# V transposed in 32x32 blocks by VectorE and reordered through DRAM instead of by TensorE

## The reference

```
xn   = group_norm(x, 32 groups)
q, k = conv1x1+affine(xn): 8 heads of 32 channels each
v4   = conv1x1+affine(xn): 1024 channels, 8 heads of 128
vl   = depthwise 3x3 convolution of v4, then an affine map
attn = q @ k^T * 32**-0.5 + bias[head, |dy|, |dx|]
attn = mix heads with th1 (8x8), softmax over the keys, mix heads with th2 (8x8)
o    = relu(attn @ v + vl)
out  = x + conv1x1+affine(o)
```

## Time and profile before

| | |
|---|---|
| time, median of 3 runs | 4813.72 us (4812.78 to 4814.12) |
| time of the profiled execution | 4811.84 us |
| its span, first to last instruction | 4810.0 us |
| mean granted clock of TensorE | 0.998 |
| busy in the span | PE 4779.1, DVE 4175.9, ACT 3251.4, POOL 988.6 us |
| DMA | 120.23 MB, 7.4% of 16 engines on SP's queue |

### The profile page before, as it was taken

The page is one execution under the profiler, slowest core; times in us unless marked ns, Lnnn a source line. Parts: engine busy times, 40 slices in busy tenths (PEclk is TensorE's granted clock), DMA queues, the critical chain, the costliest instruction groups (busy, mean ns, idle before and its releaser), DMA issues.

```text
span 4810.0 us, 111468 instructions
## 1 busy us (share of the span) xinstructions
PE 4779.1 (99%) x35842; PEld 4760.2 (99%) x35842; DVE 4175.9 (87%) x10897; ACT 3251.4 (68%) x8005; POOL 988.6 (21%) x1093
## 2 busy tenths in 40 slices
PE   7999999999999999999999999999999999999999
PEld 7999999999999999999999999999999999999999
DVE  8888888889888898888888988889888888898887
ACT  6666666666667666667666666766666766666665
POOL 3212212121121221221212212122121221221211
PEclk9999999999999999999999999999999999999999
DMA  1000000000000000000000000000000000000000
GB/s 57 26 20 30 19 26 30 15 30 25 20 30 15 30 25 20 30 15 30 30 15 30 25 20 30 15 30 25 20 30 15 30 29 16 30 21 24 30 15 26
DMA packets 55148, 120.23 MB, mean 25 GB/s; under 512 B 3650, under 2 KB 5842, under 8 KB 55124
## 3 DMA queue, kind: packets, MB, share of 16 engines
q1 hardware_dynamic: 55124, 119.93, 7.4%
HBM read 81.38 MB, written 38.54 MB: 25 GB/s over the span
## 4 chain that ended last, share of the span: by engine, by line
PE 98%; DVE 1%; issue 0%; DMA 0%; ACT 0%; SPq 0%; DVEq 0%
PE psA L250 43%; PE psA L399 14%; PE psL L250 12%; PE psM L250 10%; PE psM L377 8%; PE psL L377 6%; PE psM L367 2%; PE psL L367 2%; DVE psC L620 1%; PE psA L268 0%; PE psA L263 0%; DMA qa<-in_wqkv 0%; DVE probs L675 0%; DVE x_lo L601 0%; DVE q_lo L650 0%
## 5 line engine op out<-in xcount | busy, mean ns | idle before, releaser
L620 DVE SCALAR_TENSOR_TENSOR psC<-vpad,par,psC 128x406 f32<-128x406 f32 x3072 | 1808.7, 637 | 0.0
L498 ACT ACTIVATE probs<-probs,nmax 112x196 f32<-112x196 f32 x1792 | 799.0, 449 | 649.0 <-DVE nmax L675 641.8
L250 PE MATMUL psA<-x_hi,w_lo 128*128 128x392 f32 x2304 | 795.0, 345 | 8.5 <-DVE x_lo L601 8.5
L250 PE MATMUL psA<-x_lo,w_hi 128*128 128x392 f32 x2304 | 788.9, 342 | 0.0
L250 PE MATMUL psA<-x_hi,w_hi 128*128 128x392 f32 x2304 | 788.1, 342 | 0.0
L399 PE MATMUL psA<-qa,shared 105*128 105x196 f32 x4096 | 693.9, 330 | 3.0 <-DVE shared L719 3.0
L399 PEld LDWEIGHTS psA<-qa,shared 105*128 105x128 f32 x4096 | 680.2, 191 | 3.3 <-DVE shared L719 3.3
L650 DVE SCALAR_TENSOR_TENSOR q_lo<-q,th,q_hi 128x392 fp32r<-128x392 f32 x1024 | 604.4, 621 | 34.6 <-ACT q_hi L442 27.6
L719 DVE TENSOR_TENSOR shared<-psA,shared 128x392 f32<-128x392 f32 x512 | 290.1, 567 | 366.5 <-PE psA L399 366.5
L442 ACT ACTIVATE q_hi<-q,th 128x392 fp32r<-128x392 f32 x1024 | 582.0, 620 | 6.0
L434 ACT ACTIVATE o_hi<-shared 128x392 fp32r<-128x392 f32 x512 | 271.5, 530 | 457.6 <-DVE shared L719 457.6
(11 more groups left out here) (85 smaller groups left out, 10500.0 us busy)
## 6 DMA issues: line engine op xcount, KB each, us to landing
xs<-in_x SPq DMA_DIRECT2D x64, 588.0 KB, 3.8
shared<-in_x SPq DMA_DIRECT2D x64, 588.0 KB, 3.8
out<-shared SPq DMA_DIRECT2D x63, 588.0 KB, 3.0
qa<-in_wqkv SPq DMA_DIRECT2D x3, 768.0 KB, 6.7
stage_wp<-in_wp SPq DMA_DIRECT2D x1, 1536.0 KB, 9.9
out<-shared SPq DMA_DIRECT2D x3, 196.0 KB, 2.0
shared<-in_abx SPq DMA_DIRECT2D x1, 165.4 KB
par<-in_par SPq DMA_DIRECT2D x1, 70.5 KB
```

Source lines behind the costliest of these rows:

```text
L250: last = nc.tensor.matmul(dst, w, r, start=(begin and n == 0), stop=(end and n == 2))
L498: nc.scalar.activation(row, row, ACT.Exp, bias=nmax[:, img, b:b + 1], scale=-1.0, accum_out=rowsum[:, img, b:b + 1]).then_inc(s_exp, 1)
L620: nc.vector.scalar_tensor_tensor(a if tap == 7 else sums, src, taps[:, c, TAPS[tap]:TAPS[tap] + 1], a if tap == 0 else sums, MUL, ADD).the ...
```

## The change

TensorE's transposes, their evictions on ScalarE and `ident` are gone; the 14 mixings are left alone in the rotation of the four banks. In their place:

- VectorE runs two STREAM_TRANSPOSE instructions a pair (`turn`), one for an image. Each reads 8 groups of 224 consecutive elements of `vpad` on 128 partitions, transposes every 32x32 block by itself, and writes 1792 elements a partition into `turned` with a step of 8 elements, so that the 8 groups c are innermost. They take the places at which convs(3) stood twice.
- SP sends `turned` to a DRAM scratch `by_key`, 4 transfers for an image, one for each 32 partitions, in runs of 1 KB. When all 4 have landed it brings the rows back, 2 transfers of 112 keys by 4 KB for an image, straight into `vt`. That is 12 transfers a pair, all ahead of the store of the results in SP's order.
- `vt` is now ordered by channel and then by group, so a weight load of attn times V reads 128 elements with a step of 8.
- x_lo, q, k and k_lo share the memory of `turned` (`front`). GpSimd's x_lo of the next pair waits until image 0 has been sent out (s_vt_out[0]).
- ScalarE makes x_hi of the next pair after use 6 of 14 instead of after use 16 of 22.

```diff
@@ SP @@
+            def turned_out(t, img):
+                sp.wait_ge(s_turned, 2 * t + img + 1)
+                rows = by_key[img].rearrange("(b r) a n -> r a b n", r=BLK)
+                for a in range(P // BLK):
+                    sp.dma_start(rows[:, a, :, :],
+                                 turned[a * BLK:(a + 1) * BLK, img, :, :, :].rearrange("p b n c -> p b (n c)")
+                                 ).then_inc(s_vt_out[img], 16)
+
+            def keys_in(t, img):
+                sp.wait_ge(s_vt_out[img], 16 * (P // BLK) * (t + 1))
+                for jc in range(2):
+                    sp.dma_start(vt[0:ROWS, img, jc, :, :].rearrange("p n c -> p (n c)"),
+                                 by_key[img, jc * HALF:jc * HALF + ROWS, :, :].rearrange("k a n -> k (a n)")
+                                 ).then_inc(s_vt_in[img], 16)
...
                     load_x(t + 1)
+                turned_out(t, 0)
+                turned_out(t, 1)
+                keys_in(t, 0)
+                keys_in(t, 1)
                 if not first:
                     store(t)
@@ PE @@
-                for use in range(22):
-                    img, (what, n) = use // 11, USES[use % 11]
-                    bank_free(use)
-                    if what == "vt":
-                        jc, cg = divmod(n, 2)
-                        for c in range(4):
-                            at_ = PITCH + 1 + img * PITCH * PITCH + jc * HALF
-                            mm = nc.tensor.transpose(mix_bank(use)[:, c * P:(c + 1) * P],
-                                                     vpad[:, 4 * cg + c, at_:at_ + HALF], ident[:, :])
-                        mm.then_inc(s_vt_mm, 1)
...
-                    pe.wait_ge(s_vt_sb, 8 * t + 4 * img + 4)
+                    pe.wait_ge(s_vt_in[img], 32 * (t + 1))
                     pe.wait_ge(s_mix_sb, 14 * t + 7 * img + 7)
...
-                                                      vt[0:HALF, img, jc, g * D:(g + 1) * D], attn[:, img, jc, g, :],
+                                                      vt[0:HALF, img, jc, :, g], attn[:, img, jc, g, :],
@@ ACT @@
-                    if use == 16 and not last:
+                    if use == 6 and not last:
                         act.wait_ge(s_v_mm, VT * (t + 1))
                         x_high(t + 1)
@@ DVE @@
+                def turn(img):
+                    at_ = PITCH + 1 + img * PITCH * PITCH
+                    nc.vector.transpose(turned[:, img, :, :, :].rearrange("p b n c -> p c b n"),
+                                        vpad[:, :, at_:at_ + BLOCKS * BLK].rearrange("p c (b k) -> p c b k", b=BLOCKS)
+                                        ).then_inc(s_turned, 1)
...
-                convs(3)
+                turn(0)
                 dve.wait_ge(s_exp, 28 * t + 28)
                 nc.vector.reciprocal(rinv[:, 1, :], rowsum[:, 1, :]).then_inc(s_rinv, 1)
-                convs(3)
+                turn(1)
                 if not first:
                     project_out(t, 2)
                 convs(64)
@@ POOL @@
-                    pool.wait_ge(s_v_mm, VT * (t + 1))
+                    wait_alone(pool, s_vt_out[0], 16 * (P // BLK) * (t + 1))
                     x_low(t + 1)
```

More of the change, by code:

```diff
@@ L19 @@
 HALF = RES // 2 * PITCH
+ROWS = 112
+BLK = 32
+BLOCKS = 7
+PART = VT * BLK
 HR = P // KD
@@ L29 @@
 EPS = 1e-5
+Q_AT = 2 * CT * PIX
+K_HI_AT = Q_AT + QT * COLS
+K_AT = K_HI_AT + QT * COLS
 GAP = 2 * RES * QT * HP - VT // 2 * ACC - 4 * DH
@@ L76, in build @@
         x_hi = sb("x_hi", [P, 2, CT, PIX], f32r)
-        x_lo = sb("x_lo", [P, 2, CT, PIX], f32r)
-        q = sb("q", [P, QT, COLS])
-        k_hi = sb("k_hi", [P, QT, COLS], f32r)
-        k_lo = over("k_lo", [P, QT, COLS])
-        k = sb("k", [P, QT, COLS])
+        x_lo = over("x_lo", [P, 2, CT, PIX])
+        k_hi = over("k_hi", [P, QT, COLS], K_HI_AT)
+        k_lo = over("k_lo", [P, QT, COLS], K_AT)
+        front = sb("front", [P, 2 * BLOCKS * PART])
         q_hi = over("q_hi", [P, 2 * RES, QT, HP])
@@ L156, in build @@
         s_khi, s_klo = sem("s_khi"), sem("s_klo")
+        s_vt_out = [sem("s_vt_out0"), sem("s_vt_out1")]
+        s_vt_in = [sem("s_vt_in0"), sem("s_vt_in1")]
         s_resb, s_rstd, s_xlo, s_mixw = sem("s_resb"), sem("s_rstd"), sem("s_xlo"), sem("s_mixw")
         block = ctx.enter_context(nc.Block())
-        N_PAR_DMA = 7
+        N_PAR_DMA = 6
+        by_key = nc.dram_tensor("by_key", (2, BLOCKS * BLK, P // BLK, PART), f32, kind="Internal").ap()
         def keys(img, b):
@@ L346, in step @@
                     project(t, 2, True)
-                def bank_free(use):
+                for use in range(14):
+                    img, n = divmod(use, 7)
                     if use < 4:
                         pe.wait_ge(s_score, 28 * t + 22 + 2 * use)
-                        return
-                    i, (what, n) = (use - 4) // 11, USES[(use - 4) % 11]
-                    if what == "vt":
-                        pe.wait_ge(s_vt_sb, 8 * t + 4 * i + n + 1)
-                    else:
-                        pe.wait_ge(s_mix_sb, 14 * t + 7 * i + n + 1)
@@ new lines, in step @@
+                    else:
+                        pe.wait_ge(s_mix_sb, 14 * t + use - 3)
+                    pe.wait_ge(s_exp, 28 * t + 14 * img + 2 * n + 2)
+                    pe.wait_ge(s_mixw, 8 * t + 4 * img + group(2 * n + 1) + 1)
+                    bank = mix_bank(use)[:, 0:4 * HP].rearrange("p (j g b i) -> p j g b i", j=2, g=NH, b=2)
+                    for jc in range(2):
+                        for b in range(2):
+                            mm = nc.tensor.matmul(bank[:, jc, :, b, :],
+                                                  probs[0:HP + 1, img, 2 * n + b, jc * HALF:(jc + 1) * HALF],
+                                                  mixw[0:HP + 1, img, 2 * n + b, :].rearrange("p (g i) -> p g i", g=NH),
+                                                  start=True, stop=True)
@@ L502, in step @@
                         conv_centre(t, CENTRES[n])
-                for use in range(22):
-                    img, (what, n) = use // 11, USES[use % 11]
-                    if what == "vt":
-                        jc, cg = divmod(n, 2)
-                        act.wait_ge(s_vt_mm, 8 * t + 4 * img + n + 1)
-                        if use == 0 and not first:
-                            act.wait_ge(s_av_mm, 8 * t)
-                        nc.scalar.copy(vt[0:HALF, img, jc, cg * BANK:(cg + 1) * BANK],
-                                       mix_bank(use)).then_inc(s_vt_sb, 1)
-                    else:
-                        act.wait_ge(s_mix_mm, 14 * t + 7 * img + n + 1)
-                        src = mix_bank(use)[:, 0:4 * HP].rearrange("p (j g m) -> p j g m", j=2, g=NH)
-                        nc.scalar.copy(attn[:, img, :, :, 2 * n * RES:(2 * n + 2) * RES], src).then_inc(s_mix_sb, 1)
-                    if use == 16 and not last:
+                for use in range(14):
+                    img, n = divmod(use, 7)
+                    act.wait_ge(s_mix_mm, 14 * t + use + 1)
+                    if use == 0 and not first:
+                        act.wait_ge(s_av_mm, 8 * t)
+                    src = mix_bank(use)[:, 0:4 * HP].rearrange("p (j g m) -> p j g m", j=2, g=NH)
+                    nc.scalar.copy(attn[:, img, :, :, 2 * n * RES:(2 * n + 2) * RES], src).then_inc(s_mix_sb, 1)
+                    if use == 6 and not last:
                         act.wait_ge(s_v_mm, VT * (t + 1))
```

31 lines of the change are left out of this document (9 added, 22 removed).

## The result

The change makes the kernel slower. Its time is 5282.09 us (median of 4 runs, 5281.4 to 5284.02) beside 4813.92 us for the kernel before on the same chip, a ratio of 1.0974 [1.0955, 1.0993]. The forecast was 4920 us, in a range of 4808 to 5210: the direction is right, the size is not, and the time lies outside the range.

A forecast was written before the change was run, and what follows sets the result against it. TensorE bounds the kernel, with VectorE 3.3 us behind and taking over. VectorE's 0.1 us plus 1.6 us for the clock, times 63 pairs, adds 107 us to 4811.84: 4919, forecast 4920 us, range 4808 to 5210.

The forecast's parts named there:

- the frame: TensorE's saved 3.5 us a pair returns as a 3.6 us stop before u = 2, VectorE binding and the clock falling.
- priced at 1.6 us a pair: Granted clock falls to half behind each TensorE stop, on attn times V and the following tiles: 1.6 us a pair.
- the price of the turn by its length: VectorE's transpose of 1792 elements a partition, priced from a 1536-element row at 1.08 ns an element: 1.94, taken as 2.0 us.
- I take 2.0, by the row nearest in length: Choice of 2.0 us for each VectorE transpose, among rows giving 1.52, 1.94, 2.42 and 6.7 us.
- the forecast's own case: VectorE bounds with a falling clock, transposes of 1.94 to 2.42 us: 4862 to 5040 us, chance 0.42.
- hidden under 166 ns: Attn times V: a 128-column weight load costs 111 ns of pace, covered by 166 ns of matmul, so adds nothing.
- The rival: Attn times V: the step of 8 doubles the weight load to 221 ns, 1.77 us a step; 5085 us, chance 0.11.
- rivals that exclude each other: Slow strided write in VectorE's turn (5240 us, chance 0.17) and slow strided weight load in attn times V (5085 us, 0.11).
- a sign that it is wrong: Forecast called wrong if VectorE still waits for the first product, PE's wait ends on a DMA, or PEclk stays 1.00.
- its own count: Transfers of V: four legs of 4.8 us at 190 GB/s, image 0 in `vt` at 2473.8, in time by 1.6 us.
- The rival of late transfers: V's transfers run at 143 GB/s, 6.4 us a leg, delaying attn times V 4.3 us a pair: 5091 us, chance 0.08.
- The fast case: VectorE's transpose takes 1.52 us and the clock holds, the pair 0.86 us shorter: 4760 us, chance 0.09.

The follow-up runs named there:

- experiment 5: Kernel after with step 1 in turn and weight load (wrong channels), x_hi made after use 10 instead of 6: 4925.26 us, 1.0237.
- experiments 6 and 7: Kernel after with steps of 8 bytes and of 16 bytes instead of 32 in turn and weight load, one execution each: 5047.44 and 5249.47 us.
- Experiment 4: Kernel after without outward transfers; inward ones read other DRAM data once the logits are done, both steps of 8 kept: 5307.18 us, 1.1027.
- Experiment 13: Kernel after with 8-byte steps, image 0 turned before logits, additions between convolutions, GpSimd low parts, image 0's keys first, one inward transfer per block: 4769.33 us, 0.9907.
- experiment 12: As Experiment 13, but an image's keys come back in two transfers of 4 and 3 blocks instead of seven: 5433.29 us, 1.1292.

## Why the prediction was wrong

- **Right: the direction and the frame.** TensorE's 3.5 us a pair came back as a stop, VectorE no longer waits 3.29 us for the first product, PE's share of the chain fell, and the clock fell behind the stops. It was priced at 1.6 us a pair and cost 1.5 in the pair shown; in experiment 5, with the fast operations that the forecast assumed, 2.3. The mean granted clock is 0.957, forecast near 0.95.
- **Right: the price of the turn by its length.** 2.0 us was taken by the row of 1536 elements, and without the step it is 2.01.
- **Wrong, the step that failed: "I take 2.0, by the row nearest in length".** None of the rows it was chosen from has a step of 32 bytes. With it a turn is 3.5 us (median of 128). The 1.94 to 2.42 us that the forecast's own case allowed was too narrow for the one thing that was new in the instruction.
- **Wrong: the weight load "hidden under 166 ns".** It is not hidden: the records follow each other at 239 ns and no longer at 166 (1.91 us a step of 8, not 1.33). The rival had priced this pace at 221 ns, 1.77 us a step, which is near; the forecast's sum had this term at nothing. The 337 ns that a load takes in the profile is a duration, like the 191 before, and not to be set beside 221. Undoing this alone is worth 216 us, and undoing both steps and the place of x_hi (experiment 5) is worth 357 of the 362 us by which the forecast was off.
- **Wrong: both as rivals that exclude each other.** They were given 0.17 and 0.11 and priced one at a time. They share one cause, and experiments 6 and 7 show the same threshold in both. Priced with the measured numbers in the prediction's own way: VectorE is free at 2472.84 + 2 x 3.5 = 2479.8 and u = 2 starts at 2480.4; six steps of 1.91 in place of 1.33 add 3.5; the clock 1.5. That is 3.1 + 3.5 + 1.5 = 8.1 us a pair, 5322 us, beside 5282. So with the two sizes put right the sum comes out near, though by another path: it has the stop before u = 2, for VectorE, and in the kernel after the stop is before u = 0, for V.
- **Half right: the transfers.** The stop in the kernel after ends on a DMA, which the forecast named as a sign that it is wrong. Yet its own count has that stop: TensorE is through at 2471.15 and image 0 is in `vt` at 2473.8, 2.65 us later. It set this aside, since VectorE did not need the product before, and so moved the whole stop to u = 2. Experiment 5 shows 2.53 us there. The kernel after has 5.06: 1.7 more by the longer turn of image 0, and the three legs take 15.1 us (2447.17 to 2462.25) where 14.5 were counted. The rate was counted well. Outward transfers alone moved 225 GB/s at a DMA share of 1.00 (2450 to 2452 us), more than the 190 of the sum and the 189 that the prediction names beside it. SP needs 6.74 us for the eight issues, where 0.40 each was counted. Since the DMA engines are full in that time, no run shows that faster issues would have brought V sooner. The rival of late transfers also left out the price of the clock, 1.6 us a pair more. Experiment 4 took the lateness away and won nothing.
- **Missed: the move of x_hi.** It was not priced at all. In the kernel after the collision doesn't show. With the turns shortened it costs 2.1 us a pair. The Trainium skill's page "SBUF — State Buffer", section "Who interferes with whom", names this case: two SBUF inputs on VectorE against a GpSimd instruction that reads SBUF. Experiment 5 agrees with it: with x_lo moved away the time falls by 132 us and the group's mean is 666 ns again.
- **The fast case.** "Faster" had 0.09, by a quicker transpose. Experiment 13 shows a gain of 0.9% by another road: a step of 8 bytes, image 0 turned ahead of the logits, the additions between the last convolutions, the low parts on GpSimd, and another order and shape of the transfers. What each of these is worth by itself was not measured.

## What to carry to other kernels

Before a layout is changed for the sake of one instruction, write down the step in bytes of everything that reads or writes it, on every engine, and let the slow price of a step be one case for all of them together. When an engine is freed or a cost taken away, look at once at what lies within a microsecond behind it: here a transfer, an addition and a collision with GpSimd took each other's place. A transfer that is slow while the DMA share is small should be read by its outermost dimension first.

## What the runs showed of the hardware that was not expected

- VectorE's STREAM_TRANSPOSE of 128 x 1792 fp32 takes 2.01 us when it writes with steps of 4 or 8 bytes, 3.47 us with 16, 3.49 us with 32, and 3.60 us when it reads with 28 (medians).
- A weight load of 128 fp32 columns takes 190 ns with a step of 4 bytes, 197 with 8, 330 with 16 and 337 with 32 (medians at mostly full clock). At full clock load and product (196 columns) then follow each other at 166 ns with 4 bytes and 239 with 32; at the lower clock at 327 with either.
- Transfers with an outermost dimension of 4 and 3 held the DMA share at 0.24 and 0.18. The same bytes in pieces of 32 rows took 664 us less of the whole kernel.
- How long SP takes to issue a transfer depends on what is in flight. Eight outward transfers of 32 partitions took it 6.74 us in the kernel after, 0.84 us each, where a store of 588 KB takes it 0.41 us. In experiment 12 four of them took 10.94 us behind the slow inward ones, in experiment 13 4.04.
